# Reading column slices in place, and four moves around them, in a four-layer sequence kernel

## The reference

```
L0: U_o, V_o = gram_schmidt(U), gram_schmidt(V)      # 32 columns each
    x += strength[sample] * (x @ basis @ basis.T[:, :32] @ resp_w.T + biases)
L1: h = layer norm of x over features, then over tokens; styled by a subject's gamma, beta
    probs = softmax(h @ router_w); 2 of 8 experts per token
    x += sum of gate * (relu(h @ w1[e] + b1[e]) @ w2[e] + b2[e])
L2: one expert of 8 per sample: o = gelu(x @ Wi[e] + bi[e]) @ Wo[e] + bo[e]
    x = layer norm(o + x) * gamma[e] + beta[e]
L3: a rotation of each group of four features, by two angles of the sample
```

## Time and profile before

| what | value |
|---|---|
| median of 3 runs | 384.92 us (383.84 to 384.99) |
| profiled execution | 380.56 us, of which the span of the trace is 378.8 us |
| mean granted clock of TensorE | 0.85 |
| TensorE busy | 233.9 us (62%) |
| VectorE busy | 173.4 us (46%) |
| ScalarE busy | 129.3 us (34%) |
| GpSimd busy | 127.8 us (34%) |

### The profile page before, as it was taken

One profiled execution on the slowest core, in us unless ns is written; L12 is line 12 of the kernel. 1 busy time (PEld: TensorE's weight loads), 2 busy tenths in 40 slices (PEclk: granted clock), 3 DMA queues, 4 the chain that ended last, 5 costly groups with the idle time before them and its releaser, 6 DMA issues.

```text
span 378.8 us, 6313 instructions
## 1 busy us (share of the span) xinstructions
PE 233.9 (62%) x1440; PEld 192.8 (51%) x1440; DVE 173.4 (46%) x682; ACT 129.3 (34%) x390; POOL 127.8 (34%) x189
## 2 busy tenths in 40 slices
PE   2247788637524699676766699676465656666520
PEld 1035544623514388676655699235364656655520
DVE  4607874789639554323333355023334332352550
ACT  2203455363122256334433365024131222343310
POOL 5755500042014574222222240274334413010151
PEclk9999999956555799989999999989885665798975
DMA  1299200000022024435443443434333222241100
GB/s 32 46 315 338 83 2 1 0 0 3 0 83 54 16 73 113 106 94 109 104 97 92 110 105 95 122 74 123 87 81 99 59 87 75 58 120 60 27 28 5
DMA packets 37192, 30.07 MB, mean 79 GB/s; under 512 B 7474, under 2 KB 29788, under 8 KB 37156
## 3 DMA queue, kind: packets, MB, share of 16 engines
q1 hardware_dynamic: 31588, 18.97, 18.8%
q0 software_dynamic: 2976, 5.97, 6.1%
q10 hardware_dynamic: 2592, 4.72, 4.7%
HBM read 23.54 MB, written 5.05 MB: 75 GB/s over the span
## 4 chain that ended last, share of the span: by engine, by line
PE 23%; DMA 20%; DVE 17%; SPq 16%; issue 9%; POOL 8%; ACT 2%; ACTq 2%; POOLq 0%; DVEq 0%
DMA expert_rows<-es 11%; PE bank L986 6%; DMA big<-in_x_dram,mapx 5%; PE bank L1047 5%; SPq L386 4%; PE bank L891 2%; ACTq L727 2%; POOL big L591 2%; SPq L391 2%; SPq L380 2%; SPq L377 2%; SPq L384 2%; SPq L427 2%; DMA big<-expert_rows,sloti 1%; PE bank L1044 1%
## 5 line engine op out<-in xcount | busy, mean ns | idle before, releaser
L578 POOL DMA_INDIRECT hg<-h_rows,map x39 | 36.9, 947 | 63.9 <-PE bank L982 57.8
L986 PE MATMUL bank<-hgT,ws 128*128 128x128 f32 x312 | 44.1, 285 | 22.3 <-DVE hgT L1350 22.3
L986 PEld LDWEIGHTS bank<-hgT,ws 128*128 128x128 f32 x312 | 38.6, 195 | 27.1 <-DVE hgT L1350 26.8
L740 ACT ACTIVATE hid<-bank,bh 128x128 f32<-128x128 f32 x78 | 24.4, 363 | 61.6 <-PE bank L986 61.5
L1006 PE MATMUL bank<-w,hid 128*128 x312 | 42.3, 280 | 0.1
L591 POOL DMA_INDIRECT big<-expert_rows,sloti x32 | 31.1, 973 | 25.1 <-DMA expert_rows<-es 16.2
L1368 DVE TENSOR_TENSOR es<-bank,b2blk 128x128 f32<-128x128 f32 x39 | 11.4, 292 | 60.8 <-DMA expert_rows<-es 57.2
L1006 PEld LDWEIGHTS bank<-w,hid 128*128 128x128 f32 x312 | 38.7, 195 | 0.4 <-issue 0.3
L986 PE MATMUL bank<-hg,ws 128*128 128x128 f32 x176 | 31.7, 339 | 11.0 <-DMA hg<-big 11.0
L986 PEld LDWEIGHTS bank<-hg,ws 128*128 128x128 f32 x176 | 28.9, 249 | 12.2 <-DMA hg<-big 12.2
L1403 DVE BATCH_NORM_STATS2 st<-bank 128x6 f32<-128x128 f32 x22 | 6.6, 299 | 62.0 <-PE bank L1047 62.0
(11 more groups left out here) (321 smaller groups left out, 407.7 us busy)
## 6 DMA issues: line engine op xcount, KB each, us to landing
ws<-in_L_cond_Wi_dram ACTq DMA_DIRECT2D x18, 256.0 KB, 2.7
b2blk<-in_L_cond_exp_b_dram SPq DMA_DIRECT2D x39, 64.0 KB, 3.2
expert_rows<-es SPq DMA_DIRECT2D x39, 64.0 KB
w<-in_L_cond_exp_w_dram SPq DMA_DIRECT2D x1, 2048.0 KB, 11.0
gb<-in_L_cond_gamma_dram SPq DMA_DIRECT2D x22, 64.0 KB, 2.7
gb<-in_L_cond_beta_dram SPq DMA_DIRECT2D x22, 64.0 KB, 3.1
hg<-big SPq DMA_DIRECT2D x22, 64.0 KB, 2.3
h_rows<-big SPq DMA_DIRECT2D x4, 256.0 KB, 2.2
```

Of the source, the lines that this page charges most:

```text
L578: pool.indirect_dma_start(out=hg[:, b % RING, :], out_offset=None, in_=hdram, in_offset=bass.IndirectOffsetOnAxis(ap=map1[:, b:b + 1], axi ...
L740: last = act.activation(hid[:, u, c, :], ps[2 + u][:, c * P:(c + 1) * P], ACT.Relu, bias=bh1[:, c, b:b + 1])
L986: last = mm(ps[2 + 2 * (c // 2) + u][:, c % 2 * P:(c % 2 + 1) * P], ws[:, w, c * P:(c + 1) * P], rows, start=True, stop=True)
```

## The change

Block columns of layer 2 are no longer copied by SyncE: TensorE and ScalarE read x2T at an address held in a register. ScalarE loads all 22 starts at once before its expert numbers, TensorE one per block. The starts are computed on GpSimd during the Gram-Schmidt part. x is gathered in two batches (4 and 12 tiles), with constants between and behind them; the transposes come at later steps, and SyncE waits for all of x before it asks for w2, w1 and wo. The norm rows are fetched right after these, not in layer 1's loop. `es` has four buffers. TensorE's lag in layer 2 becomes 2, while VectorE's `combine` stays 3 ahead; ScalarE copies tile j+2 before it serves block j+1.

```diff
-LAG = 3
+LAG = 2
+LEAD = 3
-        es = sb("es", [P, 2, D])
+        es = sb("es", [P, RING, D])
-        hg2 = sb("hg2", [P, RING, P])
-        GS_XT = (4, 5, 6, 8, 9, 10, 11, 12, 13, 14, 16, 17, 18, 19, 20, 21)
-        GS_MLP = (13, 18, 20, 22, 25, 27)
-        GS_RESP = (24, 26, 28, 29)
+        GS_XT = (8, 9, 10, 11, 12, 13, 14, 16, 17, 18, 19, 20, 21, 22, 24, 25)
+        GS_MLP = (13, 18, 20, 22, 27, 29)
+        GS_RESP = (24, 26, 28, 30)
...
 SyncE:
-            sp.dma_start(w2[:], ...)
             for dst, src in ROWS: ...
+            for r in range(RING):
+                sp.wait_ge(x_ready[r], 16 * (TILES // RING))
+            sp.dma_start(w2[:], ...)
             sp.dma_start(w1[:], ...)
             sp.dma_start(wo[:], ...)
+            sp.wait_ge(oh88_ready, 1)
+            for j in range(NB2):
+                norm_rows(j)
...
-                if 2 <= b < NB2 + 2:
-                    norm_rows(b - 2)
...
-            for j in range(NB2):
-                rows_in(j, j % RING)
-                if 0 <= j - OUT_LAG < NB2 - SCATTERED:
-                    out_of_block(j - OUT_LAG)
-            for j in range(NB2 - OUT_LAG, NB2 - SCATTERED):
+            for j in range(NB2 - SCATTERED):
                 out_of_block(j)
...
 GpSimd, after 7 constants:
+            pool.wait_ge(mapx_ready, 1)
+            for i in range(RING):
+                gather_x(i)
             (tri, ones8, two iotas, masks a2 and sid)
+            for i in range(RING, TILES):
+                gather_x(i)
             (the other constants)
...
+            pool.wait_ge(oh88_ready, 1)
+            link(pool.tensor_scalar(pad2[:], nb2[:], float(SPT), None, ALU.mult))
+            link(pool.tensor_tensor(pad2[:], pad2[:], cnt2[:], ALU.subtract))
+            link(pool.tensor_tensor(cpad2[:], cmpb2[:], pad2[:]..., ALU.mult))
+            link(pool.tensor_copy(cst2f[:], io4[:]))
+            for e in range(E):
+                link(pool.tensor_tensor(cst2f[:], cst2f[:], cpad2[:, :, e], ALU.subtract))
+            pool.tensor_scalar(cst2[:], cst2f[:], float(NS), float(T), ALU.min, ALU.mult)
...
 ScalarE, before the 18 loads of expert2 and the copies of h rows:
+            act.wait_ge(cst2_ready, 1)
+            starts2 = [act.value_load(cst2[0:1, j:j + 1], ...) for j in range(NB2)]
...
-                act.wait_ge(hg2_ready[r], 16 * (j // RING + 1))
+                act.wait_ge(xT2_sb, min(j, TILES - 1) + 1)
-                act.activation(hgb[:, j % 2, :], hg2[:, r, :], ACT.Identity, bias=boT[:, j:j + 1])
+                act.activation(hgb[:, j % 2, :], x2T[:, bass.ds(starts2[j], P)], ACT.Identity, ...)
...
 TensorE:
-            pe.wait_ge(consts, N_CONST)
+            pe.wait_ge(consts, N_MEAN)
...
             def up2(j, r):
-                pe.wait_ge(hg2_ready[r], 16 * (j // RING + 1))
+                rows = block_columns(j)       # a value_load of cst2[j], then x2T[:, bass.ds(c, P)]
+                pe.wait_ge(xT2_sb, min(j, TILES - 1) + 1)
...
 VectorE:
             def sort2_counts():
+                dve.wait_ge(consts, N_SORT)
             def sort2_onehots():
+                dve.wait_ge(consts, N_CONST)
-            (five steps that computed cst2)
-                if b >= 2:
-                    dve.wait_ge(es_stored[u], 16 * (b // 2))
+                if b >= RING:
+                    dve.wait_ge(es_stored[r % RING], 16 * (b // RING))
...
-                if j + LAG < TILES:
-                    combine(j + LAG)
+                if j + LEAD < TILES:
+                    combine(j + LEAD)
```

More of the change, by code:

```diff
@@ L321, in cond_seq_kernel @@
         hg_ready = [sem(f"hg_ready{i}") for i in range(RING)]
-        es_stored = [sem(f"es_stored{i}") for i in range(2)]
+        es_stored = [sem(f"es_stored{i}") for i in range(RING)]
         x_ready = [sem(f"x_ready{i}") for i in range(RING)]
         yg_ready = [sem(f"yg_ready{i}") for i in range(RING)]
-        hg2_ready = [sem(f"hg2_ready{i}") for i in range(RING)]
         w1_ready = sem("w1_ready")
@@ L381, in bias_rows @@
                              exp_b2[bass.ds(e, 1), :].rearrange("e d -> (e d)").partition_broadcast(P)).then_inc(b2_ready[r], 16)
[L383 to L387, removed]
             def store(b, r):
                 sp.wait_ge(es_ready, b + 1)
-                sp.dma_start(edram[b * P:(b + 1) * P, :], es[:, r % 2, :]).then_inc(es_stored[r % 2], 16)
+                sp.dma_start(edram[b * P:(b + 1) * P, :], es[:, r % RING, :]).then_inc(es_stored[r % RING], 16)
             def first_weights2(b):
@@ L487, in _ @@
                                      pattern=[[1, P]], channel_multiplier=-1))
+            const(pool.memset(ones8[:], 1.0))
+            for dst, pattern, base, mult in SORT_IOTAS:
+                const(pool.iota(dst, pattern=pattern, base=base, channel_multiplier=mult,
+                                allow_small_or_imprecise_dtypes=True))
+            pool.tensor_scalar(a2f[:], iob[0:NS, 0:E], id2f[:], None, ALU.is_equal).then_inc(a2_ready, 1)
+            pool.tensor_scalar(a2[:], iob[0:NS, 0:E], id2f[:], None, ALU.is_equal).then_inc(a2_ready, 1)
+            link(pool.tensor_copy(idf[:], id1[:]))
+            pool.tensor_scalar(sid[:], idf[:], pidx[0:SUBJ, :], None, ALU.is_equal).then_inc(sid_ready, 1)
+            for i in range(RING, TILES):
+                gather_x(i)
             const(pool.memset(onesrow[:], 1.0))
@@ L501, in _ @@
             assert count[0] == N_CONST
[L503 to L513, removed]
-                    in_offset=bass.IndirectOffsetOnAxis(ap=mapx[:, i:i + 1], axis=0)).then_inc(x_ready[i % RING], 16)
             pool.wait_ge(ld_small, 16 * N_SMALL)
@@ L582, in _ @@
                     pool.memset(x2T[:, NT:NT + P], 0.0).then_inc(x2pad_ready, 1)
-            pool.wait_ge(es_stored[0], 16 * ((NB1 + 1) // 2))
-            pool.wait_ge(es_stored[1], 16 * (NB1 // 2))
+            for r in range(RING):
+                pool.wait_ge(es_stored[r], 16 * len(range(r, NB1, RING)))
             def gather_y(i):
@@ L725, in _ @@
             act.activation(trig[:], angw[:], ACT.Sin).then_inc(trig_ready, 1)
+            act.wait_ge(cst2_ready, 1)
+            starts2 = [act.value_load(cst2[0:1, j:j + 1], min_val=0, max_val=NT) for j in range(NB2)]
             for j in range(RING, NB2):
@@ L775, in residual2 @@
             def residual2(j, r):
[L776 removed]
+                act.wait_ge(xT2_sb, min(j, TILES - 1) + 1)
                 if j >= 2:
                     act.wait_ge(down2_ps, j - 1)
[L779 removed]
+                act.activation(hgb[:, j % 2, :], x2T[:, bass.ds(starts2[j], P)], ACT.Identity, bias=boT[:, j:j + 1]).then_inc(hgb_ready, 1)
             def hidden2(j, r):
@@ L796, in _ @@
                 columns2(i)
-            for j in range(NB2):
-                residual2(j, j % RING)
-                hidden2(j, j % RING)
+            residual2(0, 0)
+            hidden2(0, 0)
+            for j in range(NB2 - 1):
                 if j + LAG < TILES:
                     columns2(j + LAG)
+                residual2(j + 1, (j + 1) % RING)
+                hidden2(j + 1, (j + 1) % RING)
         @block.tensor
@@ L1035, in up2 @@
                     pe.wait_ge(hid2_sb, j - 1)
-                up_product(r % 2, w, hg2[:, r, :]).then_inc(up2_ps, 1)
+                up_product(r % 2, w, rows).then_inc(up2_ps, 1)
             def down2(j, r):
@@ L1445, in _ @@
             dve.wait_ge(gb_ready, 32 * NB2)
-            for i in range(LAG):
+            for i in range(LEAD):
                 combine(i)
             for j in range(NB2 + 2):
-                if j + LAG < TILES:
-                    combine(j + LAG)
+                if j + LEAD < TILES:
+                    combine(j + LEAD)
                 if j < NB2:
```

81 lines of the change are left out of this document (45 added, 36 removed).

## The result

The changed kernel takes 308.69 us (median of 4 runs, 308.08 to 311.14); the kernel before took 384.38 beside it (379.06 to 384.99). The ratio is 0.8105, with a 95% interval of 0.7988 to 0.8221. The forecast was 316, with a range of 304 to 335. The execution profiled took 311.14 us with a span of 309.4; the sum of the prediction had 309.5 for this span. Of the four executions the profiled one was the longest; the spans of the others are 306.3 to 307.5.

The account below looks back on a forecast made before the run. Waits bound it: late gathers at the start, SyncE's queue in layer 1, a ring in layer 2. Span 378.8 -8.5 +11.7 -30.5 -45.0 +3 = 309.5; +1.76 gives 311.3, +4.36 gives 315.6, said as 316; range 304 to 335.

Parts of the forecast that it names:

- start (fold): Gram-Schmidt start: earlier gathers of x and later transposes shrink VectorE's 10.28 us stop; -8.5 us, bounds -10.2 and -4.
- routing (the ranks behind it): After the logits: 22 more ScalarE register loads at 0.53 us lie on the path; +11.7 us, bounds 11 and 13.
- layer 1, first to last result: Layer 1: SyncE's step falls to 1.5 us, TensorE sets 1.89 a block; -30.5 us, bounds -30.5 to -11.
- G to the end, with the clock's 3: Layer 2 from its first gather of results (G): 136.1 to 91.1 us, saving 45.0, less 3 allowed for the clock.
- median of the runs over the profiled execution: Whole kernel: the runs' median of 384.92 lay 4.36 us above the profiled execution, so 4.36 was added to 311.3.
- Rival 3: Start: gives nothing, as the recursion meets late constants or transposes elsewhere; +8.5 us, about 324; chance 0.08.
- rival 5: Routing: ScalarE's register loads overlap by half and no clock is lost; about 306 us; chance 0.07.
- Rival 2: Layer 1: bound by transfers, three of 64 KB a block, 2.4 us each block; +19, about 335 us; chance 0.08.
- rival 4: Layers 1 and 2: clock falls to half as products become dense; slower, about 405 us; chance 0.02.
- the ring: Layer 2: cycle of down product, statistics, combine, transpose, up product; 7.87 us in the pair shown; LAG 2 breaks it.
- GpSimd's order: Layer 2: power, two gathers, next power become what is late next; 6.9 us a turn of two blocks.
- Rival 1: Layer 2: half clock throughout, end 115.5 us after its first gather of results; about 337 us; chance 0.13.

## Why the prediction was right, term by term

| term | predicted | measured in the profile after |
|---|---|---|
| start (fold) | -8.5 | -9.3 |
| routing (the ranks behind it) | +11.7 | +11.9 |
| ranks to the first result | 0 | 24.5 to 24.4: -0.1 |
| layer 1, first to last result | -30.5 | 102.3 to 71.1: -31.2 |
| last result to G | 0 | 3.5 to 6.2: +2.7 |
| G to the end, with the clock's 3 | -42.0 | 136.1 to 92.7: -43.4 |
| span | 309.5 | 309.4 |
| median of the runs over the profiled execution | +4.36 | -2.45 |

The last term was mis-sized. The prediction added to its 311.3 the 4.36 us by which the median of before lay above its profiled execution, as if that were a constant. The profiled execution of the changed kernel took 311.14, and the median lies 2.45 below it. Runs of before spread from 379.06 to 384.99, so the profiled 380.56 was a quick one of its kind. These two, 4.36 and 2.45, are nearly the whole error of 7.3 us.

That the span came out within 0.1 us is luck in two ways. The four stages gained 2.7 us more than was summed, and the way of the last store into layer 2, which the sum left at nothing, took 2.7 back. And the profiled execution was the longest of four; the others would have made it 2 to 3 us less.

*Start.* The size was right and the weight of its parts was not. The prediction held late gathers responsible and let the new steps of the transposes follow; the run with the old order shows that the steps do nearly all of it (7.9 of 9.3 us at the first boundary). Rival 3 (the start gives nothing) is refuted by 53.3 here; on the experiments' chips the fold moved only from 62.0 to 59.4.

*Routing.* 22 x 0.53 on the path held to 0.2 us, and the removal of the wait by moving the loads shows that nothing hid the new ones; rival 5 (loads that overlap) is out. The floor that the Trainium skill gives for such a load (DMA: Bandwidth & Descriptors, Latency and other measured facts) would have made it 13.2, an estimate; the measured 11.9 goes with the 0.53 of the row.

*Layer 1.* Rival 2 (bound by transfers) is refuted: three transfers of 64 KB a block, 1.87 us an interval, DMA share 0.51. TensorE is the bound, and its clock stayed at 1.00, which refutes rival 4. Of the two reasons given only one counts, the norm rows; the result buffers were not needed. One thing it did not foresee: the last store took 4.49 us to land, where it took 2.97 before, so G came 6.2 us after the last result and not 3.5.

*Layer 2.* The first turn was 6.9 as predicted, and the mean of the first six is 7.2 (233.33 to 276.47); the fifth power came at G+46.1 and not G+43.1, and from there to the end it took 46.6 and not 48.0. The 3 us allowed for the clock covered the difference. The tail after the last statistics is 16.7.

The mechanism is only half right. The prediction had the ring broken by the lag, and GpSimd's order (power, gathers, landing) as what is late next. The run with the power later took the gathers off and the turn stayed at 7.6 us: a ring over TensorE and VectorE is still there, two blocks long. In the chain of the changed kernel both appear, the power and its gather at 233.33 and 262.82, and VectorE's scaling at 248.54 and 256.19 with no gather between. The two rings are within 1 us of each other, so that the turn of 6.9 came near was in part luck.

The prediction let the lag carry the gain and said that the slice copies vanish in it. The runs show 16 to 20 us for the lag with the copies in place. Without the lag, the slices in place gain 10 us in the tail and lose them again in the middle, at a lower clock. The clock does not explain the lag's own gain, which came at 0.80 in both runs; whether a shorter way into a product and more time at the full level feed each other when both edits stand was not tried apart. Rival 1 (half clock) did not come with this lag. With lag 3 and slices in place the clock was near half (0.62), and the layer took 40.6 us more than in the changed kernel: some 21 us of that is the longer ring in the middle (60.1 against 39.1, at clocks of 0.80 and 0.85), and 12.5 go with the lower clock.

*Open.* On these chips the changed kernel's span is 14.5 us longer, most of it beside pauses without a releaser, so the ratio there is 0.83 and not 0.81. In the start they came with the changed code where the weights are held, and stayed when the whole old order was put back; with only the weights let go they were gone. Whether the instructions came late or a semaphore did, the trace doesn't say, and no run separates the two.

## What to carry to other kernels

A queue that issues transfers is an engine with a pace: add up what stands in it for one block, before giving more buffers to those who wait for it. A register load before the one instruction that all wait for cost its full half microsecond here once nothing covered it; put it where its engine waits anyway. Two edits in the same stage can be worth little alone and much together, so undo each from both sides, and cut the traces at the same event: a total of nothing can be a gain in one part and a loss in the next. When a ring is said to be broken, look for the next longer one through the same engines. And don't take the distance of one profiled execution from a median for a constant.

## What the hardware showed that was not expected

- The first norm row stood 10.67 us in its issue on SyncE (45.26), behind the requests for three weights of 2 MB; its successors took mostly 0.33 to 0.38. The prediction had these rows done near 80; they were done at 90.5, and the 22 us left before SyncE's next duty covered it.
- The same kernel took 308.69 us beside the kernel before at 384.38, and 325.88 on chip 8 beside 392.66. Where the difference lies, the traces have waits of 1 to 10 us that nothing in them released; the one in the start shows on TensorE and VectorE at once.
- The granted clock fell to 0.60 in a stretch of 8 us in which TensorE was busy 7.63, after one in which it was busy 5.66 of 8 at 0.97.
